# Turning the packed down weights late: all tiles in batch 12, their scaling on GpSimd in the last three batches

## The chip, the cores and the metric

The kernel runs on one core of one Trainium2 chip. The metric is the device time of one execution in microseconds (us); the kernel before took 838.14 us as the median of three runs (835.20, 838.14 and 841.78). One profiled execution gives all rows below.

## What is computed

A gated cross-attention layer and a gated feed-forward layer over 16 batches of `[128, 512]` float32:

```python
x = x + tanh(g_xattn) * attention(layernorm(x), ctx)      # 8 heads, projections mix the 128 rows
x = x + tanh(g_ffn) * ffn(layernorm(x))                   # 512 -> 2 x 1408 -> 512, then RMS norm

nib  = packed >> (4 * arange(8)) & 15                     # 8 weights of 4 bits in a word
vals = FP4_LUT[nib]                                       # 0, .5, 1, 1.5, 2, 3, 4, 6 and their negatives
w    = vals * repeat(scales, 128)                         # one fp16 scale per output and 128 inputs
h = silu(x @ w_gate.T) * (x @ w_up.T);  y = h @ w_down.T
```

Only the dequantization of `w_down` (512 x 1408, as 11 tiles of 128 x 512) is touched. Its result, a rounded head `dn_head` and the rest `dn_rest`, is first read in the feed-forward part, after all attention is done.

## The kernel before, in words

Two blocks run one after the other, with a barrier of all engines between them: `attend` (batches 0 to 15, up to about 490 us) and `feed_forward` (4 groups of 4 batches, 11 tiles each, to the end). Each engine has its instructions in a fixed order, written out by hand; semaphores tie them together.

In `attend`, a batch is 16 slots. In slot s of batch b, TensorE computes scores of batch b + 1 (L437), which VectorE reduces to row maxima (L699, `maxima`), and at the same time the transposed scores of batch b (L449), which ScalarE exponentiates (L556), and their product with the values (L467). So VectorE's maxima are always one batch ahead. The score results go through two buffers in turn, so TensorE can be two scores ahead of VectorE at most. VectorE also turns the maxima into rows (`turn_max`, L705, L707, L711) in slot 0 and slot 7, inverts the softmax sums of the batch before in slot 6 (`invert_sums`, L716), and in batch 15, in which it has no maxima, turns the gate and up weights in slots 1 to 6 (six operations of 1408 words, L720, L724, L728).

SyncE issues nearly all transfers, in one written order per batch (`sync_step`). Its late part matters here. In step b it stores the maxima of batch b (L260), loads them back (L266), gathers the sums of batch b - 1 (L274) and merges its quads (L280), then `store_x(b - 2)` (L298), which waits until the residual of batch b - 2 is added, then `store_inverse(b - 1)` (L285), `store_max(b + 1, 0)` (L260), its load (L266), `load_inverse(b - 1)` (L291), and `gather_sums(b, 0)` (L274). After step 15 come `gather_sums(15, 1)`, `merge_quads(15)`, `store_x(14)`, `store_inverse(15)`, `load_inverse(15)`, `store_x(15)`. What stands behind a waiting transfer in this order waits with it.

GpSimd runs `pool_step(b)`: `residual(b - 2)` (L662), the rotation and splitting of the projections of batch b + 3 while there are such (b below 13), `scale_heads(b - 1)` (L657), which waits for the inverse sums that SyncE loads (L291), and last `scale_down` for one tile. `residual(14)` stands after step 15; VectorE does batch 15's own.

The down weights travel so before: in batches 0 to 10 SyncE loads one tile of packed words (`load_down`, L348); in batches 1 to 11 it loads the tile's scales, spread over 128 partitions (`load_down_scale`, L303), into one of two buffers, and in slots 13 to 15 VectorE turns the bits of one tile, in three operations of 128 words (`turn_nibbles`): a shift of the upper half (L720), a mask and shift into `magnitude` (L724), a combination (L728). After that an fp8 view of the words gives the values. In steps 2 to 12 GpSimd does `scale_down` of one tile: product with the scales (L837), cast to the head (L839), the rest (L841).

Of the kernel before, what the change touches and what calls it, by code (L numbers as in the profile page):

```python
# [7 lines left out]
ALU = mybir.AluOpType  # L8
# [5 lines left out]
F16 = mybir.dt.float16  # L14
# [3 lines left out]
P = 128  # L18
B = 16
T = 512  # L20
# [5 lines left out]
IT = INNER // P  # L26
# [13 lines left out]
GU_COLS = 2 * INNER  # L40
GU_WORDS, DN_WORDS = KT * GU_COLS // 4, IT * T // 4
BIT_STEPS = 3
DN_AT, GU_AT = 2, 3
X_GAIN = 2.0 ** 11

SLOTS = 2 * QUADS * KT
# [51 lines left out]
def attend(nc, d, keep):  # L98
    with ExitStack() as ctx:
        sb = lambda name, shape, dt: ctx.enter_context(nc.sbuf_tensor(name, shape, dt))  # L100
        ps = lambda name, shape, dt: ctx.enter_context(nc.psum_tensor(name, shape, dt))
        sem = lambda name: ctx.enter_context(nc.semaphore(name))
        two = range(2)
# [36 lines left out]
        gu_bits, dn_bits = keep["gu_bits"], sb("dn_bits", [P, DN_WORDS], U32)  # L140
        magnitude = sb("magnitude", [P, DN_WORDS], U32)
        gu_sc16 = sb("gu_sc16", [P, KT, GU], F16)
        dn_sc16 = [sb(f"dn_sc16_{p}", [P, T], F16) for p in two]
        dn_full = sb("dn_full", [P, T], F32)

        st_ps = [ps(f"st_ps{r}", [P, T], F32) for r in range(ST_BANKS)]
# [9 lines left out]
        scales_in = sem("scales_in")  # L156
        gu_in = sem("gu_in")
        dn_in = sem("dn_in")
        dn_sc_in = [sem(f"dn_sc_in{p}") for p in two]
        x_in = [sem(f"x_in{n}") for n in range(X_TILES)]  # L160
        c_in = [sem(f"c_in{n}") for n in range(C_TILES)]
        consts = sem("consts")
# [3 lines left out]
        dn_turned = sem("dn_turned")  # L166
        gu_turned = sem("gu_turned")
        dn_product = sem("dn_product")
# [40 lines left out]
        turn = lambda n: n // 2 + 1  # L209
# [4 lines left out]
        with nc.Block() as block:  # L214
# [83 lines left out]
                sp.dma_start(keep["x_dram"][b], xt[b % X_TILES][:]).then_inc(x_stored[b % 2], 16)  # L298

            def load_down_scale(sp, t):  # L300
                if t >= 2:
                    sp.wait_ge(dn_product, t - 1)
                sp.dma_start(dn_sc16[t % 2][:], d["down_scales"][t].rearrange("(a h) -> a h", a=1).to_broadcast([P, T])).then_inc(dn_sc_in[t % 2], 16)  # L303

            def sync_step(sp, b):
                nxt, proj_n = b + 1 < B, b + AHEAD_PROJ
# [368 lines left out]
            def head_rot(dve, n):  # L675
                dve.wait_ge(rotated, n + 1)
                if n:
                    dve.wait_ge(stored[0], PARTS * n)
                nc.vector.tensor_copy(split_head[:, 0], swap[:]).then_inc(rot_head, 1)
# [7 lines left out]
            def take_v(dve, n):  # L687
                item = S_NO["v", n]
                dve.wait_ge(s_full, item + 1)
                if n >= 2:  # L690
                    dve.wait_ge(pv_done, (n - 1) * SPANS)
                out = v_ones[n % 2][:].rearrange("p k j q (a c) -> p (k j) (q a) c", a=2)[:, :, 0:4:3, :]
                nc.vector.tensor_copy(out, s_ps[item % S_BANKS][:, 0, :].rearrange("p (x q c) -> p x q c", q=QUADS, c=KC)).then_inc(s_read, 1)

            def maxima(dve, n, slot):
                item = S_NO["score", n, slot]
                j, qt = score_of(slot)
                dve.wait_ge(s_full, item + 1)
                nc.vector.tensor_reduce(neg_max[j // 2][:, :, j % 2, qt], s_ps[item % S_BANKS][:], AXIS_X, ALU.max,  # L699
                                        negate=True).then_inc(s_read, 1)  # L700

            def turn_max(dve, n, h):
                dve.wait_ge(s_read, S_NO["score", n, (h + 1) * SLOTS // QUADS - 1] + 1)
                maximum = neg_max[h][:].rearrange("p o j k -> p (o j k)")
                nc.vector.tensor_copy(max_rows[h][:, 0], maximum).then_inc(max_head[h], 1)  # L705
                dve.wait_ge(max_head[h], n + 1)
                nc.vector.tensor_tensor(max_rows[h][:, 1], maximum, max_rows[h][:, 0].bitcast(F32), ALU.subtract).then_inc(max_rest[h], 1)  # L707
                dve.wait_ge(max_rest[h], n + 1)
                if n:
                    dve.wait_ge(max_out[h], 16 * n)  # L710
                nc.vector.transpose(max_lines[h][:].bitcast(F32), max_rows[h][:].bitcast(F32).rearrange("p r i -> p (r i)")).then_inc(max_line[h], 1)  # L711

            def invert_sums(dve, b):
                for h in two:
                    dve.wait_ge(sums_in[h], 16 * (b + 1))
                nc.vector.reciprocal(sums[:], sums[:]).then_inc(inverses, 1)  # L716

            def turn_nibbles(dve, words, step, at, done, turned):
                if step == 0:
                    nc.vector.tensor_scalar(words[halves[0], at], words[halves[0], at], 4, None,  # L720
                                            ALU.logical_shift_left).then_inc(turned, 1)
                elif step == 1:
                    dve.wait_ge(turned, done + 1)
                    nc.vector.tensor_scalar(magnitude[:, 0:at.stop - at.start], words[:, at], 0x70707070, 1, ALU.bitwise_and,  # L724
                                            ALU.logical_shift_right).then_inc(turned, 1)
                else:
                    dve.wait_ge(turned, done + 2)
                    nc.vector.scalar_tensor_tensor(words[:, at], words[:, at], 0x80808080, magnitude[:, 0:at.stop - at.start],  # L728
                                                   ALU.bitwise_and, ALU.bitwise_or).then_inc(turned, 1)

            def vector_step(dve, b):
                proj_n = b + AHEAD_PROJ
                for slot in range(SLOTS):
                    if b + 1 < B:
                        maxima(dve, b + 1, slot)
                        if slot == V_AT:
                            take_v(dve, b + 1)
                    elif 1 <= slot <= 2 * BIT_STEPS:
                        if slot == 1:
                            dve.wait_ge(gu_in, 16 * 2 * KT)  # L740
                        piece, step = divmod(slot - 1, BIT_STEPS)
                        turn_nibbles(dve, gu_bits, step, slice(piece * DN_WORDS, (piece + 1) * DN_WORDS), BIT_STEPS * piece, gu_turned)
                    if slot == 0:
                        turn_max(dve, b, 1)
                    if slot == 3 and b + 4 < B:
                        statistics(dve, b + 4)
                    if slot == 6 and b:
                        invert_sums(dve, b - 1)
                    if slot == 7 and b + 1 < B:
                        turn_max(dve, b + 1, 0)  # L750
                    if slot == 7 and proj_n < B:
                        head_pass(dve, proj_n)
                    if slot == 11 and proj_n < B:
                        head_rot(dve, proj_n)
                    if slot >= SLOTS - BIT_STEPS and 1 <= b <= IT:
                        t = b - 1
                        dve.wait_ge(dn_in, 32 * b)
                        turn_nibbles(dve, dn_bits, slot - (SLOTS - BIT_STEPS), slice(t * T // 4, b * T // 4), BIT_STEPS * t, dn_turned)

            @block.vector  # L760
            def _(dve):
# [52 lines left out]
            def pool_step(pool, b):  # L814
                proj_n = b + AHEAD_PROJ
                if b >= 2:
                    residual(pool, nc.gpsimd, b - 2)
                if proj_n < B:
                    rotate_own(pool, nc.gpsimd, proj_n)
                    rotate_partner(pool, nc.gpsimd, proj_n)  # L820
                    rest_pass(pool, nc.gpsimd, proj_n)
                if b + 4 < B:
                    normalise(pool, nc.gpsimd, b + 4)
                if proj_n < B:
                    rest_rot(pool, nc.gpsimd, proj_n)
                if b:
                    scale_heads(pool, nc.gpsimd, b - 1)
                if DN_AT <= b < DN_AT + IT:
                    scale_down(pool, b - DN_AT)

            def scale_down(pool, t):
                pool.wait_ge(dn_turned, BIT_STEPS * (t + 1))
                if t:
                    pool.wait_ge(dn_rested, t)
                pool.wait_ge(dn_sc_in[t % 2], turn(t) * 16)
                vals = dn_bits[:].bitcast(FP8E3)[:, t * T:(t + 1) * T]
                nc.gpsimd.tensor_tensor(dn_full[:], vals, dn_sc16[t % 2][:], ALU.mult).then_inc(dn_product, 1)  # L837
                pool.wait_ge(dn_product, t + 1)
                nc.gpsimd.tensor_copy(keep["dn_head"][:, t, :], dn_full[:]).then_inc(dn_headed, 1)  # L839
                pool.wait_ge(dn_headed, t + 1)  # L840
                nc.gpsimd.tensor_tensor(keep["dn_rest"][:, t, :], dn_full[:], keep["dn_head"][:, t, :].bitcast(F32),  # L841
                                        ALU.subtract).then_inc(dn_rested, 1)
# [454 lines left out]
```

## Time and profile before

| | |
|---|---|
| median of 3 runs | 838.14 us (835.20 to 841.78) |
| profiled execution, its own time | 833.57 us |
| span of its instructions | 831.8 us |
| TensorE busy | 719.3 us (86%) |
| VectorE busy | 622.9 us (75%) |
| ScalarE busy | 531.9 us (64%) |
| GpSimd busy | 376.5 us (45%) |
| mean granted TensorE clock | 0.93 of full speed |

TensorE is busy nearly throughout, but "busy" includes matmuls that wait for the pace of others. Shares over the span mix two blocks with different limits, so the stretches below are cut at the starts of TensorE's first score (L437) of a batch: batch 3 starts at 131.81 us, batch 7 at 242.92, batch 8 at 267.98, batch 9 at 300.23, batch 12 at 382.52, batch 13 at 407.67, batch 14 at 431.57, batch 15 at about 454. The attention's last store is issued at 490.03 us, and the feed-forward block's first load at 490.77 us.

### The profile page before, as it was taken

How to read it: one execution, taken by the hardware profiler on the slowest of the kernel's cores; microseconds unless marked ns; L12 is line 12 of the kernel's file. 1: busy time of each engine (PE TensorE's matmuls, PEld its weight loads, DVE VectorE, ACT ScalarE, POOL GpSimd, SP SyncE). 2: the span in 40 equal slices, each digit the busy share in tenths (PEclk: the TensorE clock that was granted, in tenths of full speed). 3: DMA queues.
4: the chain of work that ended last, by engine and by line, in shares of the span. 5: the costliest groups of instructions: out<-in, count | busy, mean ns of one | idle time of the engine just before them, and what ended most of it. 6: DMA issues, size and time to landing. Idle time of an engine off the chain costs nothing. (4 is left out here: it accounts for less than half of the span.)

```text
span 831.8 us, 13555 instructions
## 1 busy us (share of the span) xinstructions
PE 719.3 (86%) x4660; PEld 338.8 (41%) x4660; DVE 622.9 (75%) x879; ACT 531.9 (64%) x965; POOL 376.5 (45%) x298
## 2 busy tenths in 40 slices
PE   3369999889999999999999805998998999889995
PEld 1124334333334334333344303554554555555553
DVE  5588999979889869898999316766677677776774
ACT  2217888768868658788788805565566457465744
POOL 2123344445444425454401102676558655955662
PEclk9559999999989859999999957999999999999999
DMA  6655677766776666666632140000000200000011
GB/s 212 196 154 164 148 191 199 203 158 179 197 215 184 160 172 172 165 184 183 177 95 63 38 159 36 1 0 2 1 0 26 77 0 1 27 25 1 1 39 63
DMA packets 55113, 88.74 MB, mean 107 GB/s; under 512 B 16901, under 2 KB 20357, under 8 KB 55045
## 3 DMA queue, kind: packets, MB, share of 16 engines
q1 hardware_dynamic: 54320, 87.68, 37.9%
q8 instruction: 37, 0.61, 0.3%
q10 hardware_dynamic: 724, 0.20, 0.1%
q14 instruction: 32, 0.25, 0.1%
HBM read 46.95 MB, written 34.34 MB: 98 GB/s over the span
## 5 line engine op out<-in xcount | busy, mean ns | idle before, releaser
L556 ACT ACTIVATE probs<-st_ps 128x512 f32<-128x512 f32 x512 | 277.2, 595 | 108.9 <-PE st_ps L449 97.9
L699 DVE TENSOR_REDUCE neg_max<-s_ps 128x2 f32<-128x1024 f32 x256 | 303.8, 1214 | 38.3 <-PE s_ps L437 37.7
L1075 POOL TENSOR_TENSOR pair<-parts 128x512 f32<-128x512 f32 x88 | 116.3, 1325 | 135.7 <-ACT parts L1095 135.7
L467 PE MATMUL pv_ps<-probs,v_ones 128*32 128x256 f32 x2048 | 168.9, 403 | 0.8 <-ACT pv_sb L562 0.8
L437 PE MATMUL s_ps<-k_stack,q_stack 48*128 48x512 f32 x512 | 137.3, 533 | 34.5 <-DVE neg_max L699 29.4
L1200 PE MATMUL gu_ps<-x_head,gu_bits 128*128 128x512 f16 x352 | 136.3, 387 | 19.3 <-ACT parts L1095 16.8
L1200 PE MATMUL gu_ps<-x_rest,gu_bits 128*128 128x512 f16 x352 | 135.4, 385 | 0.0
L1095 ACT ACTIVATE parts<-gu_ps,gu_sc 128x512 f32<-128x512 f32 x176 | 111.5, 680 | 10.6 <-PE gu_ps L1200 10.6
L449 PE MATMUL st_ps<-q_stack,k_stack 50*128 50x512 f32 x512 | 112.1, 424 | 0.0
L437 PEld LDWEIGHTS s_ps<-k_stack,q_stack 48*128 48x128 f32 x512 | 50.9, 196 | 148.8 <-DVE neg_max L699 72.5
L962 DVE SCALAR_TENSOR_TENSOR up<-gu_ps,gu_sc,up 128x512 f32<-128x512 f32 x132 | 98.6, 747 | 8.0 <-PE gu_ps L1200 4.2
L1102 ACT ACTIVATE silu<-gate 128x512 f32<-128x512 f32 x44 | 27.7, 630 | 109.7 <-POOL gate L1079 109.6
L959 DVE TENSOR_SCALAR up<-gu_ps,gu_sc 128x512 f32<-128x512 f32 x44 | 33.0, 751 | 68.4 <-PE gu_ps L1200 68.3
L467 PEld LDWEIGHTS pv_ps<-probs,v_ones 128*32 128x32 f32 x2048 | 41.1, 109 | 102.1 <-ACT probs L556 75.9
L1216 PE MATMUL y_ps<-dn_head,h_head 128*128 128x512 f32 x176 | 77.5, 440 | 4.4 <-DVE y_sb L1011 3.9
L1200 PEld LDWEIGHTS gu_ps<-x_head,gu_bits 128*128 128x128 fp8e3 x352 | 34.5, 98 | 86.3 <-ACT parts L1095 35.4
L1216 PE MATMUL y_ps<-dn_rest,h_head 128*128 128x512 f32 x176 | 69.4, 395 | 0.0
L1216 PE MATMUL y_ps<-dn_head,h_rest 128*128 128x512 f32 x176 | 69.3, 394 | 0.0
L449 PEld LDWEIGHTS st_ps<-q_stack,k_stack 50*128 50x128 f32 x512 | 63.9, 194 | 9.7 <-issue 4.4
L1079 POOL TENSOR_TENSOR gate<-pair 128x512 f32<-128x512 f32 x44 | 58.9, 1339 | 3.5
L657 POOL TENSOR_TENSOR heads_out<-pv_sb,scale_of 128x512 f32<-128x512 f32 x15 | 19.4, 1295 | 84.3 <-DMA scale_of<-inverse_scratch 84.3
L1200 PEld LDWEIGHTS gu_ps<-x_rest,gu_bits 128*128 128x128 fp8e3 x352 | 34.9, 99 | 30.7 <-issue 1.9
(109 smaller groups left out, 816.2 us busy)
## 6 DMA issues: line engine op xcount, KB each, us to landing
q_stack<-image SPq DMA_DIRECT2D x64, 192.0 KB, 3.5
k_stack<-image SPq DMA_DIRECT2D x64, 192.0 KB, 4.5
image<-split_head SPq DMA_DIRECT2D x32, 256.0 KB
image<-split_head SPq DMA_DIRECT2D x64, 128.0 KB
image<-split_rest SPq DMA_DIRECT2D x32, 256.0 KB
ct<-ctx_dram SPq DMA_DIRECT2D x16, 256.0 KB, 6.3
swap<-proj SPq DMA_DIRECT2D x64, 64.0 KB, 2.7
scale_of<-inverse_scratch SPq DMA_DIRECT2D x16, 256.0 KB
```

The source lines that it names most:

```text
L437: last = nc.tensor.matmul(out[:, odd, :], q_stack[p][rows, j, qt * P:(qt + 1) * P], k_stack[p][rows, j, :], start=True, stop=True)
L449: nc.tensor.matmul(out[:], k_stack[p][rows, j, kt * P:(kt + 1) * P], q_stack[p][rows, j, :], start=True, stop=True).then_inc(st_full, 1)
L467: last = nc.tensor.matmul(pv_ps[2 * KC * j:2 * KC * (j + 1), cols], v_ones[b % 2][:, kt, j, quad, :], probs[at % PROBS][:, j, cols], start ...
L556: nc.scalar.activation(probs[at % PROBS][:, tile % 4, :], st_ps[item % ST_BANKS][:], ACT.Exp).then_inc(st_read, 1)
L699: nc.vector.tensor_reduce(neg_max[j // 2][:, :, j % 2, qt], s_ps[item % S_BANKS][:], AXIS_X, ALU.max, negate=True).then_inc(s_read, 1)
L959: nc.vector.tensor_scalar(out, bank, scale, None, ALU.mult).then_inc(up_read, 1)
L962: nc.vector.scalar_tensor_tensor(out, bank, scale, out, ALU.mult, ALU.add).then_inc(up_read, 1)
L1075: nc.gpsimd.tensor_tensor(pair[:, n], parts[T_ % 2][:, 2 * n], parts[T_ % 2][:, 2 * n + 1], ALU.add).then_inc(pairs_ok, 1)
L1079: nc.gpsimd.tensor_tensor(gate[T_ % 2][:], pair[:, 0], pair[:, 1], ALU.add).then_inc(gate_ok, 1)
L1095: nc.scalar.activation(parts[T_ % 2][:, k], gu_ps[(2 * k) % BANKS][:], ACT.Copy, scale=gu_sc[:, k, T_ % IT:T_ % IT + 1]).then_inc(gate_rea ...
L1200: last = nc.tensor.matmul(gu_ps[n % BANKS][:], gu_vals[:, k, col:col + P], moving[g % 2][:, k], start=first, stop=not first)
L1216: last = nc.tensor.matmul(y_ps[:, j, :], h[T_ % H_RING][:, cols], keep[w][:, t, :], start=(t == 0 and n == 0), stop=(t == IT - 1 and n == 2))
```

## The change

The words of all 11 tiles stay packed until slots 13 to 15 of batch 12, where three operations turn them all (1408 words each). GpSimd scales and splits four tiles in step 13, four in step 14 and three in step 15, each time after `scale_heads`. The scales of all tiles get a buffer of their own, so loading them waits for nothing; the loads keep their places in SyncE's order.

```diff
-DN_AT, GU_AT = 2, 3
+DN_AT, DN_TILES, GU_AT = 13, 4, 3
...
-        dn_sc16 = [sb(f"dn_sc16_{p}", [P, T], F16) for p in two]
+        dn_sc16 = sb("dn_sc16", [P, IT, T], F16)
...
             def load_down_scale(sp, t):
-                if t >= 2:
-                    sp.wait_ge(dn_product, t - 1)
-                sp.dma_start(dn_sc16[t % 2][:], d["down_scales"][t].rearrange("(a h) -> a h", a=1).to_broadcast([P, T])).then_inc(dn_sc_in[t % 2], 16)
+                sp.dma_start(dn_sc16[:, t, :], d["down_scales"][t].rearrange("(a h) -> a h", a=1).to_broadcast([P, T])).then_inc(dn_sc_in, 16)
...
-                    if slot >= SLOTS - BIT_STEPS and 1 <= b <= IT:
-                        t = b - 1
-                        dve.wait_ge(dn_in, 32 * b)
-                        turn_nibbles(dve, dn_bits, slot - (SLOTS - BIT_STEPS), slice(t * T // 4, b * T // 4), BIT_STEPS * t, dn_turned)
+                    if slot >= SLOTS - BIT_STEPS and b == DN_AT - 1:
+                        dve.wait_ge(dn_in, 32 * IT)
+                        turn_nibbles(dve, dn_bits, slot - (SLOTS - BIT_STEPS), slice(0, DN_WORDS), 0, dn_turned)
...
-                if DN_AT <= b < DN_AT + IT:
-                    scale_down(pool, b - DN_AT)
+                if b >= DN_AT:
+                    for t in range(DN_TILES * (b - DN_AT), min(IT, DN_TILES * (b - DN_AT + 1))):
+                        scale_down(pool, t)
...
             def scale_down(pool, t):
-                pool.wait_ge(dn_turned, BIT_STEPS * (t + 1))
+                pool.wait_ge(dn_turned, BIT_STEPS)
                 if t:
                     pool.wait_ge(dn_rested, t)
-                pool.wait_ge(dn_sc_in[t % 2], turn(t) * 16)
+                pool.wait_ge(dn_sc_in, 16 * (t + 1))
                 vals = dn_bits[:].bitcast(FP8E3)[:, t * T:(t + 1) * T]
-                nc.gpsimd.tensor_tensor(dn_full[:], vals, dn_sc16[t % 2][:], ALU.mult).then_inc(dn_product, 1)
+                nc.gpsimd.tensor_tensor(dn_full[:], vals, dn_sc16[:, t, :], ALU.mult).then_inc(dn_product, 1)
```

## Rows read from the trace of the kernel before

**Rows 1.** Windows by batch: stretch, its us, busy by engine, clock, DMA share, GB/s

```profile
131.81:382.52 250.71, 235.92 (x1894) 94.07 (x1890) 216.20 (x289) 187.53 (x352) 114.31 (x100) 0.93 0.68 183
242.92:267.98 25.06, 24.37 (x214) 9.90 (x211) 22.91 (x33) 20.80 (x40) 12.09 (x11) 1.00 0.65 186
267.98:300.23 32.25, 30.50 (x215) 11.51 (x211) 25.69 (x33) 21.27 (x41) 14.97 (x13) 0.78 0.73 193
382.52:407.67 25.15, 24.33 (x214) 9.72 (x211) 22.62 (x28) 20.51 (x38) 11.85 (x10) 1.00 0.61 169
407.67:431.57 23.90, 22.25 (x206) 9.50 (x203) 22.16 (x25) 19.12 (x36) 6.39 (x6) 1.00 0.49 124
```

**Rows 2.** Groups of instructions of VectorE: the turning of one tile, eleven times

```profile
L728 DVE SCALAR_TENSOR_TENSOR dn_bits<-dn_bits,magnitude 128x128 uint32<-128x128 uint32 x11 | 4.5, 407 | 0.0
L724 DVE TENSOR_SCALAR magnitude<-dn_bits 128x128 uint32<-128x128 uint32 x11 | 3.4, 308 | 0.0
L720 DVE TENSOR_SCALAR dn_bits<-dn_bits 64x128 uint32<-64x128 uint32 x11 | 2.3, 208 | 0.0
```

**Rows 3.** Timeline, VectorE and GpSimd, slot 0 of batch 13: start, us, what

```profile
408.79 1.28 POOL L657 TENSOR_TENSOR heads_out<-pv_sb,scale_of 128x512 f32<-128x512 f32 x1 [4.57 <-DMA scale_of<-inverse_scratch]
409.36 0.74 DVE L705 CAST max_rows<-neg_max 128x16 fp32r<-128x16 f32 x1
410.03 1.10 POOL L837 TENSOR_TENSOR dn_full<-dn_bits,dn_sc 128x512 f32<-128x512 fp8e3 x1
410.13 1.03 DVE L707 TENSOR_TENSOR max_rows<-neg_max,max_rows 128x16 fp32r<-128x16 f32 x1
411.19 0.61 POOL L839 CAST dn_head<-dn_full 128x512 fp32r<-128x512 f32 x1
411.19 0.21 DVE L711 STREAM_TRANSPOSE max_lines<-max_rows 128x32 f32<-128x32 f32 x1
411.88 1.28 POOL L841 TENSOR_TENSOR dn_rest<-dn_full,dn_head 128x512 fp32r<-128x512 f32 x1
```

**Rows 4.** Timeline, VectorE, slot 0 of batch 14

```profile
433.67 0.21 DVE L711 STREAM_TRANSPOSE max_lines<-max_rows 128x32 f32<-128x32 f32 x1
```

**Rows 5.** Waits: who waited for what, us in total, times, longest

```profile
DVE sums L716 <- DMA sums<-pv_sb: 18.2, 6, 14.1
```

**Rows 6.** Timeline, VectorE and GpSimd, batch 15: turning 1408 words of `gu_bits`

```profile
455.41 0.84 DVE L720 TENSOR_SCALAR gu_bits<-gu_bits 64x1408 uint32<-64x1408 uint32 x1
457.22 1.62 DVE L728 SCALAR_TENSOR_TENSOR gu_bits<-gu_bits,magnitude 128x1408 uint32<-128x1408 uint32 x1
459.67 0.89 DVE L724 TENSOR_SCALAR magnitude<-gu_bits 128x1408 uint32<-128x1408 uint32 x1
460.30 1.40 POOL L662 TENSOR_TENSOR xt<-xt,attn 128x512 f32<-128x512 f32 x1 [9.00 <-ACT attn L571]
460.60 2.59 DVE L728 SCALAR_TENSOR_TENSOR gu_bits<-gu_bits,magnitude 128x1408 uint32<-128x1408 uint32 x1
```

**Rows 7.** Timeline, GpSimd and SyncE's queue, from step 13's end to the attention's end

```profile
430.70 1.28 POOL L657 TENSOR_TENSOR heads_out<-pv_sb,scale_of 128x512 f32<-128x512 f32 x1 [14.16 <-DMA scale_of<-inverse_scratch]
443.86 0.50 SPq L260 DMA_DIRECT2D max_scratch<-max_lines  x1
446.43 0.64 SPq L291 DMA_DIRECT2D scale_of<-inverse_scratch  x1
450.02 1.28 POOL L657 TENSOR_TENSOR heads_out<-pv_sb,scale_of 128x512 f32<-128x512 f32 x1 [10.63 <-DMA scale_of<-inverse_scratch]
469.55 1.28 POOL L657 TENSOR_TENSOR heads_out<-pv_sb,scale_of 128x512 f32<-128x512 f32 x1 [7.85 <-DMA scale_of<-inverse_scratch]
478.91 0.52 SPq L298 DMA_DIRECT2D x_scratch<-x_last  x1
479.48 1.24 SPq L285 DMA_DIRECT2D inverse_scratch<-sums  x2
481.93 0.64 SPq L291 DMA_DIRECT2D scale_of<-inverse_scratch  x1
```

More of the change, by code:

```diff
@@ L158, in attend @@
         dn_in = sem("dn_in")
-        dn_sc_in = [sem(f"dn_sc_in{p}") for p in two]
+        dn_sc_in = sem("dn_sc_in")
         x_in = [sem(f"x_in{n}") for n in range(X_TILES)]
```

## The prediction

> **What bounds the kernel now.** I read the 40 slices of the profile first (they show where attention ends and the feed-forward block starts), then the windows cut at each batch, then the timeline of VectorE, GpSimd and SyncE's queue around the lines that move. The change touches nothing after 490.77 us, where the feed-forward block starts; all of its effect is on when attention ends.
>
> In the windows an undisturbed batch takes 25.06 us, and batch 12, in which VectorE turns no down weights at all, takes 25.15 us [rows 1]. So in an undisturbed batch the turning is worth nothing: TensorE and ScalarE set a slot's pace, and VectorE's three small operations fit in front of the next score. But nine batches (3 to 11) take 250.71 us together, 25.2 us more than 9 x 25.06; batch 8 alone takes 32.25 us at a granted clock of 0.78, a mixture of both levels, 1.2 and 2.4 GHz [rows 1]. In these VectorE waits in slot 6 for the sums that SyncE gathers [rows 5], scores pile up, and the clock falls behind such a gap.
>
> At the other end, after batch 13, GpSimd has almost nothing to do, but what it does stands on a chain: residual, `store_x`, `store_inverse`, `load_inverse`, `scale_heads`, one turn per batch, because SyncE issues in a fixed order. In the last turn the inverse of batch 15 is issued right behind `store_x(14)` (478.91, then 479.48), and everything to the end of attention hangs on it [rows 7].
>
> **The change, part by part.**
>
> *Removed from VectorE in batches 1 to 11:* 33 operations, 2.3 + 3.4 + 4.5 = 10.2 us busy [rows 2]. Taken at nothing directly, covered by the score's own pace as said.
>
> *Removed from GpSimd in steps 2 to 12:* eleven tiles. GpSimd had time for them, but they got in VectorE's way. In slot 0 of batch 13 a cast that should be short took 0.74 us, ending with GpSimd's L657, and the subtraction L707 took 1.03 us, ending as L837 ends; the transpose L711 started 3.52 us after the batch, against 2.10 us (433.67 - 431.57) in batch 14, where GpSimd was idle [rows 1, 3, 4]. So up to 1.42 us came off the store of the maxima in each such batch, and behind this store stands the gathering of the sums. The bounds: a gain of nothing, if the landing of the transfers decides (SyncE issues as many as before), and of all 25.2 us, if every disturbed batch becomes an undisturbed one. I take 4.1 us, the five waits for sums during the loop (18.2 - 14.1, the last being the wait at the end) [rows 5], because a store that is at most 1.4 us earlier reaches that far and no further: **-4.1**.
>
> *Loads of scales:* as many, at the same places in SyncE's order; the wait that goes was for a product two batches old. Nothing.
>
> *Added to VectorE in slots 13 to 15 of batch 12:* three operations of the size of the gate and up turns: 0.84 (L720), 0.89 (L724) and 1.62 us (L728), 3.35 us; up to 1 us more if GpSimd is in the way, as in the L728 that took 2.59 us [rows 6]. A maximum behind each of them waits, and with two score buffers TensorE is held soon after. Batch 13 no longer has the 1.42 us of interference, of which the part by `scale_heads` (about 0.6 us) stays [rows 3]. Nothing later in the loop gives the delay back, since TensorE's slot is then no shorter: 3.35 - 0.85 = **+2.5** (bounds +1.5 and +4.5: part of it hidden by the buffers, or both blockings in full).
>
> *Added to GpSimd in steps 13 to 15:* tiles. One costs by the spacing of starts 1.16 + 0.69, then 1.28 and the gap to the next, which I estimate from the two earlier gaps at 0.07: 3.20 us [rows 3]. Now the chain on the old clock times [rows 3, 6, 7]:
> - `scale_heads(12)` at 430.70, first tile 1.24 us later, four tiles to 444.7, then `residual(12)` to 446.0. SyncE's `store_x(12)` waits for it, and behind it `store_inverse(13)` (0.57 + 1.24), `store_max(15, 0)` and from there 2.57 us to `load_inverse(13)`: 450.4. It was 446.43.
> - `scale_heads(13)` 3.59 us later, at 454.0 (was 450.02). Four tiles: 1.24 + 12.8, to 468.1 if undisturbed.
> - These run just when VectorE turns the gate and up weights. GpSimd's L662 began at 460.30 while VectorE's L724 ran until 460.56, and took 1.40 us where its kind takes 1.28; the L728 behind it stood until GpSimd had finished (2.59 us against 1.62) [rows 3, 6]. So they take turns, and each VectorE operation that runs holds GpSimd for its length less about 0.13. Six of them, 2 x 3.35 = 6.7, less 0.8: 5.9 us more, to 474.0. `residual(13)` to 475.3.
> - `store_x(13)` 475.3, to `load_inverse(14)` 3.02 us (478.91 to 481.93), 478.3; `scale_heads(14)` 3.59 later, 481.9; three tiles, 1.24 + 9.6, to 492.8; `residual(14)` to 494.1, `store_x(14)` at 494.1. It was at 478.91: **+15.2**.
>
> VectorE and TensorE have room behind this chain: the merges of batch 15 were issued before `store_x(14)` at 478.91, so even 5 us later they don't decide. What is late next is only `store_inverse(15)` itself.
>
> The Trainium skill (SBUF — State Buffer, Who interferes with whom) has the loser of the port pair that GpSimd and VectorE share block fully, for the whole instruction of the other. By the rule six whole operations, 6.7 us, would be added instead of 5.9, and the sum would be 0.8 us higher; the trace agrees in kind and is a little milder.
>
> The Trainium skill (Perfetto Trace Analysis, the notes under the GPSIMD instruction) warns that a GpSimd span in a profile is unreliable and that start-to-start spacing is to be used. By the spans (1.10 + 0.61 + 1.28) a tile would be 2.99 us, and eleven tiles 2.3 us less than by the spacing that I take.
>
> **Sum.** -4.1 + 2.5 + 15.2 = +13.6 us. On the profiled execution's own 833.57 us this is 847.2. That execution was faster than all three runs shown, whose median is 838.14; on that it is 851.7. I predict against the median: **851 us**.
>
> **Rivals.**
> - *The turns don't hold GpSimd.* If VectorE's six operations fit beside the tiles, or fall before them, the last term is 15.2 - 5.9 = 9.3 and the sum +7.7: 846 us. Against it is the 1.40 us row; for it, that it is one row with an overlap of 0.26 us [rows 6]. Chance 0.2.
> - *The loop gives back more than the tail takes.* The mechanism: in slot 0 of batches 3 to 12 the maxima leave up to 1.42 us sooner, the sums are there in slot 6, and neither the wait nor the fall of the clock behind it comes. If all 25.2 us go: +17.7 - 25.2 = -7.5, 831 us. It decides where more than 17.7 of the 25.2 us come back. For it: the undisturbed batches show that the clock is whole (1.00) wherever VectorE doesn't stall [rows 1]. Against: SyncE has no transfer less to issue. Chance 0.12.
> - *A fall of the clock more.* VectorE's 3.35 us in batch 12 hold TensorE longer than any wait in rows 5 but the last; if the clock falls as in batch 8, whose excess over 25.06 was 7.2 us, and half to all of this comes on top: +17 to +21, 857 us. Chance 0.1.
> - *The change moves nothing of weight*, because the tail is covered by something later than the sums' inverse: I see nothing there; 838 us. Chance 0.03.
>
> My forecast has 0.55.
>
> **How the numbers follow.** The forecast's own range is 847 to 856 (recovery of 0 to 8 us, the turn between +1.5 and +4.5). The range to the first and third rival is 840 to 858; left out are the second and fourth rival and something above. A measurement of this kernel tells about 1% (8.4 us) from no change. Slower by more than that, above 846.5: nearly all of the forecast, half of the first rival, the third: 0.72. Faster, below 829.8: only the second rival at its very end, 0.04. Within: 0.24.
>
> **What would show it.** In the profile after: L716 no longer waits in the loop, and the batches 3 to 12 are shorter by some us in all; three long VectorE operations in batch 12 and TensorE waiting for L699 there; GpSimd without a gap from its L657 in steps 13, 14 and 15 through the tiles; its operations in batch 15 lengthened beside L720, L724 and L728; `store_x(13)` and `store_x(14)` waiting for GpSimd's L662, the latter about 15 us later than the end of the merges would allow; the feed-forward stretch as long as before. I am wrong if `store_x(14)` doesn't wait, or if batches 3 to 12 shrink by 10 us and more.

## The result

The changed kernel is slower: 859.10 us median (854.76 to 862.93, four runs) against 839.96 us (835.20 to 842.29, four runs), a ratio of 1.0234 with a 95% interval of 1.0158 to 1.0309. That is 19 us where 13 were forecast, 1.1 us above the end of the range. The kernel before has one execution more here than when the prediction was made, and its median is 1.8 us higher for it. Here and below, medians take in every execution, while ratios leave out the slow ones, those more than 1.5% above the fastest of their kernel. The changed kernel's profiled execution took 854.76 us, its span is 852.6 us against 831.8.

### The profile page after: what moved, and what is told of

It is laid out like the page before. It is cut to its first block and busy times, and to the rows that moved or that the text cites. A ratio compares the mean times of both kernels' runs of the same rounds, so it can differ in the third digit from the quotient of the medians.

```text
span 852.6 us, 13505 instructions
## 1 busy us (share of the span) xinstructions
PE 728.8 (85%) x4660; PEld 342.5 (40%) x4660; DVE 620.9 (73%) x849; ACT 531.3 (62%) x965; POOL 381.1 (45%) x298
## 5 line engine op out<-in xcount | busy, mean ns | idle before, releaser
L1093 ACT ACTIVATE parts<-gu_ps,gu_sc 128x512 f32<-128x512 f32 x176 | 111.5, 678 | 11.6 <-PE gu_ps L1198 11.5
L435 PEld LDWEIGHTS s_ps<-k_stack,q_stack 48*128 48x128 f32 x512 | 51.2, 197 | 152.0 <-issue 73.0
L655 POOL TENSOR_TENSOR heads_out<-pv_sb,scale_of 128x512 f32<-128x512 f32 x15 | 19.6, 1308 | 81.3 <-DMA scale_of<-inverse_scratch 81.3
```

What stands on the lines that cost most here:

```text
L435: last = nc.tensor.matmul(out[:, odd, :], q_stack[p][rows, j, qt * P:(qt + 1) * P], k_stack[p][rows, j, :], start=True, stop=True)
L1093: nc.scalar.activation(parts[T_ % 2][:, k], gu_ps[(2 * k) % BANKS][:], ACT.Copy, scale=gu_sc[:, k, T_ % IT:T_ % IT + 1]).then_inc(gate_rea ...
```

## The profile after

The same stretches as in [rows 1], from the changed kernel's windows (stretch, us, busy by engine, clock, DMA share, GB/s): batches 3 to 11, and batch 13.

```profile
132.52:385.19 252.67, 237.85 (x1894) 95.13 (x1890) 208.93 (x262) 187.23 (x352) 86.81 (x72) 0.91 0.71 182
410.38:437.10 26.72, 23.95 (x203) 9.73 (x203) 23.43 (x27) 18.99 (x35) 3.00 (x2) 0.94 0.45 111
```

GpSimd did 86.8 us of work in batches 3 to 11 instead of 114.3, and VectorE 208.9 instead of 216.2, but they took 252.67 us instead of 250.71 [rows 1]. Batch 13 took 26.72 us instead of 23.90.

The chain at the end, which answers to [rows 7] (timeline, GpSimd and SyncE's queue; L655 is `scale_heads`, L660 the residual, L298 `store_x`):

```profile
437.13 1.28 POOL L655 TENSOR_TENSOR heads_out<-pv_sb,scale_of 128x512 f32<-128x512 f32 x1 [15.25 <-DMA scale_of<-inverse_scratch]
451.39 1.29 POOL L660 TENSOR_TENSOR xt<-xt,attn 128x512 f32<-128x512 f32 x1
460.55 1.28 POOL L655 TENSOR_TENSOR heads_out<-pv_sb,scale_of 128x512 f32<-128x512 f32 x1 [7.87 <-DMA scale_of<-inverse_scratch]
479.28 1.28 POOL L660 TENSOR_TENSOR xt<-xt,attn 128x512 f32<-128x512 f32 x1
487.23 1.26 POOL L655 TENSOR_TENSOR heads_out<-pv_sb,scale_of 128x512 f32<-128x512 f32 x1 [6.67 <-DMA scale_of<-inverse_scratch]
498.01 1.26 POOL L660 TENSOR_TENSOR x_last<-x_last,attn 128x512 f32<-128x512 f32 x1
...
499.30 0.34 SPq L298 DMA_DIRECT2D x_scratch<-x_last  x1
```

No residual here has an idle time in brackets: GpSimd came to each straight from a tile. From `scale_heads(12)` to `store_x(14)` it is 499.30 - 437.13 = 62.17 us; before it was 478.91 - 430.70 = 48.21 [rows 7].

The two engines beside each other in batch 15 (VectorE's turning of the gate and up weights, and GpSimd's tiles, in two answers of the timeline):

```profile
463.08 1.21 DVE L718 TENSOR_SCALAR gu_bits<-gu_bits 64x1408 uint32<-64x1408 uint32 x1
464.33 1.86 DVE L722 TENSOR_SCALAR magnitude<-gu_bits 128x1408 uint32<-128x1408 uint32 x1
466.22 2.41 DVE L726 SCALAR_TENSOR_TENSOR gu_bits<-gu_bits,magnitude 128x1408 uint32<-128x1408 uint32 x1
468.56 1.29 DVE L718 TENSOR_SCALAR gu_bits<-gu_bits 64x1408 uint32<-64x1408 uint32 x1
...
463.63 1.80 POOL L839 TENSOR_TENSOR dn_rest<-dn_full,dn_head 128x512 fp32r<-128x512 f32 x1
465.57 1.58 POOL L835 TENSOR_TENSOR dn_full<-dn_bits,dn_sc 128x512 f32<-128x512 fp8e3 x1
467.21 1.89 POOL L837 CAST dn_head<-dn_full 128x512 fp32r<-128x512 f32 x1
469.18 1.82 POOL L839 TENSOR_TENSOR dn_rest<-dn_full,dn_head 128x512 fp32r<-128x512 f32 x1
```

A cast of 0.61 us takes 1.89, a product of 1.10 takes 1.58, a rest of 1.28 takes 1.80 (the shorter ones in [rows 3]), and the VectorE operations are longer than the undisturbed ones in [rows 6] too: the six together run from 463.08 to 474.20, 11.1 us for what takes 6.7 alone.

The whole difference of 20.8 us of span, cut at the same events in both traces (one execution of each kernel, so that the loop's row, above all, holds their spread too):

| stretch | before, us | after, us | difference | forecast |
|---|---|---|---|---|
| to batch 3 | 131.81 | 132.52 | +0.7 | 0 |
| batches 3 to 11 | 250.71 | 252.67 | +2.0 | -4.1 |
| batch 12 to `scale_heads(12)` | 48.18 | 51.94 | +3.8 | +2.5 |
| `scale_heads(12)` to `store_x(14)` | 48.21 | 62.17 | +14.0 | +15.2 |
| to the feed-forward's first load | 11.86 | 11.68 | -0.2 | 0 |
| feed-forward | 341.03 | 341.62 | +0.6 | 0 |

## The experiments

Two theories stood after the result. **A**: the loss is the long turn in batch 12 and the tail, and the loop (batches 3 to 11) gains nothing because something in SyncE's or the DMA engines' work sets its pace. **D**: taking GpSimd's tiles out of the loop is worth the 4.1 us forecast, and something else loses more. Ratios are to the kernel before, on the same chip.

**Turning early, scaling late**

```diff
-                    if slot >= SLOTS - BIT_STEPS and b == DN_AT - 1:
-                        dve.wait_ge(dn_in, 32 * IT)
-                        turn_nibbles(dve, dn_bits, ..., slice(0, DN_WORDS), 0, dn_turned)
+                    if slot >= SLOTS - BIT_STEPS and 1 <= b <= IT:
+                        t = b - 1
+                        dve.wait_ge(dn_in, 32 * b)
+                        turn_nibbles(dve, dn_bits, ..., slice(t * T // 4, b * T // 4), BIT_STEPS * t, dn_turned)
```

> The changed kernel, but VectorE turns one tile in each of batches 1 to 11 as before (slots 13 to 15), and only GpSimd's scaling is late. Theory A (the loss has two places: the three long VectorE operations in batch 12 cost 3.7 us up to scale_heads(12), and GpSimd's tiles ahead of the residuals cost 14 us behind it): about 4 us less than the changed kernel, so 15 to 16 us over the kernel before, 855 us; batch 13 back at about 24 us. Rival B (the long operations only fill a gap in VectorE, the loss is all in the tail): no different from the changed kernel, 859 us. Rival C (turning per batch costs time in the loop, which the change had saved): slower than the changed kernel, 861 us or more.

Measured: 860.0 us, ratio 1.0207 (1.0116 to 1.0298): the time alone doesn't tell it from the changed kernel. Its windows do:

```profile
135.55:400.24 264.69, 249.32 (x1894) 97.16 (x1890) 211.33 (x289) 187.31 (x352) 86.72 (x72) 0.86 0.66 173
425.73:448.43 22.70, 22.18 (x206) 9.60 (x203) 20.74 (x25) 18.91 (x36) 3.29 (x3) 1.00 0.50 130
```

Batch 13 took 22.70 us, 4.0 less than with the late turn, but this execution's loop took 12 us more, at a clock of 0.86. The loop varies by more than the term that I wanted to see. Whether turning per batch makes it longer (rival C) this run leaves open; it stands against it that of f1 and f2 below, which both have the same loads moved, the one that turns per batch (f2) has the shorter loop, 244.1 us against 254.2.

**The same tiles, in GpSimd's gaps**

```diff
+                for t in {14: (2, 3), 15: (7, 8)}.get(b, ()):
+                    scale_down(pool, t)
                 if b:
                     scale_heads(pool, nc.gpsimd, b - 1)
-                if b >= DN_AT:
-                    for t in range(DN_TILES * (b - DN_AT), min(IT, DN_TILES * (b - DN_AT + 1))):
-                        scale_down(pool, t)
+                for t in {13: (0, 1), 14: (4, 5, 6), 15: (9, 10)}.get(b, ()):
+                    scale_down(pool, t)
```

> The changed kernel with the same eleven late tiles on GpSimd in another order: two after scale_heads(12), then residual(12), two, scale_heads(13), three, residual(13), two, scale_heads(14), two, residual(14). No residual then waits for more than one or two tiles. Theory A: the chain residual, store_x, store_inverse, load_inverse, scale_heads is nearly free again; of the 14 us behind scale_heads(12) at most 3 stay (two tiles before scale_heads(13) and (14), each stretched by VectorE's turning of the gate and up weights), so about 12 us less than the changed kernel, 5 to 7 us over the kernel before, 846 us. Rival B (GpSimd's total work late is what costs, wherever it stands): 857 us, as the changed kernel.

Measured: 848.18 us, ratio 1.0080 (1.0037 to 1.0123). 1.5% of the 2.3% came back without a tile less: most of what costs is where the tiles stand in the order, not GpSimd's work. From `scale_heads(12)` to `store_x(14)` it was 52.64 us:

```profile
435.32 1.28 POOL L655 TENSOR_TENSOR heads_out<-pv_sb,scale_of 128x512 f32<-128x512 f32 x1 [14.76 <-DMA scale_of<-inverse_scratch]
...
487.96 0.34 SPq L298 DMA_DIRECT2D x_scratch<-x_last  x1
```

**No work on the down weights.** The kernel leaves out the turning and the scaling and fills the weights with a constant, so its result is not the layer's; the loads stay.

```diff
-                        turn_nibbles(dve, dn_bits, ..., slice(0, DN_WORDS), 0, dn_turned)
...
-                        scale_down(pool, t)
+                if b < 2:
+                    nc.gpsimd.memset(keep[("dn_head", "dn_rest")[b]][:].bitcast(F32), 0.25).then_inc(dn_product, 1)
```

> The changed kernel without the turning and the scaling of the down weights: dn_head and dn_rest are filled with a constant by two memsets of GpSimd in steps 0 and 1, the loads of words and scales stay. It bounds what all this work costs. Theory A (in the kernel before, the work was free, because SyncE's issuing sets the pace of batches 3 to 11): the time of the kernel before within 2 us, 838 to 842 us. Rival D (the step of the prediction: interference of GpSimd with VectorE in slot 0 cost 4.1 us): 4 us less than the kernel before, 836 us. With the changed kernel as measure, 18 to 20 us less by A, 23 by D.

Measured: ratio 0.9993 (0.9938 to 1.0049); the median of all ten executions is 848.92 us against 841.87. In the kernel before, turning and scaling cost nothing that this run can tell from zero. The interval reaches 5.2 us down, so it does not by itself exclude D's 4.1.

**Gate and up loads out of the loop** (on the kernel before)

```diff
-                if GU_AT <= b < GU_AT + 2 * KT:
-                    load_gate_up(sp, b - GU_AT)
+                if b in (12, 13):
+                    for n in range(4 * (b - 12), 4 * (b - 11)):
+                        load_gate_up(sp, n)
```

> The kernel before with one thing changed: the eight loads of packed gate and up weights leave steps 3 to 10 of SyncE's order and stand in steps 12 and 13, four each, where SyncE has fewer transfers to issue. Theory A (in batches 3 to 10 SyncE's issue of about 42 transfers, some 25.7 us, and their landing are what makes every second batch late): each batch gains about 0.6 us of issue and the queue ahead of the maxima is shorter, so the long batches mostly vanish; 5 to 20 us less than the kernel before, 828 us. Rival E (the long batches come from VectorE's and GpSimd's work, not from SyncE): no change, 838 to 841 us.

Measured: 830.55 us, ratio 0.9879 (0.9787 to 0.9971). Moving eight transfers that nobody waits for until batch 15 gains what moving eleven tiles of real work did not:

```profile
135.59:377.75 242.16, 227.64 (x1890) 90.71 (x1890) 218.65 (x288) 186.65 (x350) 113.56 (x99) 0.96 0.69 182
```

The loop took 242.16 us instead of 250.71, with one long fall of the clock left (batch 6, 32.6 us), and VectorE's waits for the sums in it come to 0.5 us instead of 4.1:

```profile
DVE sums L717 <- DMA sums<-pv_sb: 14.6, 2, 14.1
```

**The changed kernel in the calmer loop, and both mends there.** The first is the changed kernel with the edit of the last experiment; the second has besides the early turn of the first and the gaps of the second experiment.

> The changed kernel with the gate and up loads in steps 12 and 13, as in e4_gate_up_loads_late, to whose 830.6 us it is to be compared: the loop varies less there. Theory A (the loss is the long turn in batch 12, 3.7 to 4.8 us, and the tail behind scale_heads(12), 14 us): 18 us over e4, 849 us; from scale_heads(12) to store_x(14) 62 us against 46.6 in e4. Rival F (part of the loss measured for the change is more falls of the clock in the loop, which the calmer loop doesn't have): 13 us over e4 or less, 843 us.

Measured: ratio 1.0124 (1.0071 to 1.0177), 850.57 us. From `scale_heads(12)` (444.82) to `store_x(14)` (507.02) it was 62.20 us, as A said. Its profiled execution was the longest of its ten, 861.69 us.

> As f1_after_calm, with both mends: VectorE turns one tile per batch in batches 1 to 11, and GpSimd's tiles stand in its gaps, as in e2_tiles_in_gaps. Theory A (two places, additive): of the 18 us the turn's 4 and 10 of the tail's 14 come back, 835 us, 4 to 5 over e4. Rival C (turning one tile per batch costs the loop what the late turn saves): 839 us.

Measured: ratio 0.9946 (0.9905 to 0.9988), 836.62 us. The two mends together are worth 1.8%, and 14 us by the medians of the two, where A said 14. From `scale_heads(12)` (429.80) to `store_x(14)` (479.20) it was 49.40 us. Batch 13 of the two (f1, then f2):

```profile
415.94:443.49 27.55, 25.12 (x203) 10.04 (x204) 23.53 (x27) 19.07 (x36) 2.59 (x2) 0.88 0.60 147
...
404.30:427.55 23.25, 22.27 (x208) 9.52 (x204) 20.84 (x25) 18.90 (x36) 2.56 (x2) 1.00 0.69 168
```

Again about 4 us for the late turn, and with it the clock below 1. Batch 7 of f1 took 31.26 us at a clock of 0.82 although VectorE did not wait in its slot 6: a late sum is not the only thing that stands before a fall. Rival F is not confirmed: against e4's ratio of 0.9879, f1 is 2.5% slower, no less than the change cost at first.

**The gate and up turn after the tiles** (on the changed kernel)

```diff
+                dve.wait_ge(gu_in, 16 * 2 * KT)
+                dve.wait_ge(dn_rested, 8)
+                for n in range(2 * BIT_STEPS):          # after batch 15's slots, not in slots 1 to 6
+                    piece, step = divmod(n, BIT_STEPS)
+                    turn_nibbles(dve, gu_bits, step, slice(piece * DN_WORDS, (piece + 1) * DN_WORDS), ...)
```

> The changed kernel, but VectorE turns the gate and up weights after batch 15's slots, once GpSimd has finished eight tiles, instead of beside tiles 4 to 7. Theory A (the two engines take turns, so six VectorE operations lengthen GpSimd's tiles): the four tiles 4 to 7 take 13 us instead of 17.5, and the time from scale_heads(12) to store_x(14) is 57.5 us instead of 62.2. Rival (they don't block each other, the tiles are long for another reason): 17 us and 62 us as before.

Measured in a single execution, 852.75 us (timeline, GpSimd):

```profile
463.82 1.28 POOL L655 TENSOR_TENSOR heads_out<-pv_sb,scale_of 128x512 f32<-128x512 f32 x1 [7.88 <-DMA scale_of<-inverse_scratch]
477.97 1.28 POOL L660 TENSOR_TENSOR xt<-xt,attn 128x512 f32<-128x512 f32 x1
```

`scale_heads(13)`, its four tiles and the start of the residual took 14.15 us, against 18.73 us in the changed kernel (479.28 - 460.55); from `scale_heads(12)` (440.39) to `store_x(14)` (497.89) it was 57.50 us, against 62.17. So 4.6 us of the tail were VectorE and GpSimd in each other's way. The time of the whole tells nothing here.

**Fewer transfers, same bytes in all** (on e4)

```diff
-                if b < IT:
-                    load_down(sp, b)
-                if 1 <= b <= IT:
-                    load_down_scale(sp, b - 1)
+                if b == 0:
+                    load_down(sp)                       # all words, two transfers
+                if b in (1, 4, 8):
+                    load_down_scales(sp, {1: 0, 4: 4, 8: 8}[b])
```

> The kernel before with the gate and up loads in steps 12 and 13 and the down weights' transfers merged: all packed words in two transfers in step 0 (22 before), the scales in three, in steps 1, 4 and 8 (11 before); turning and scaling as in the kernel before. Theory A (SyncE's issuing and the queue it fills pace batches 2 to 11): SyncE then has slack in every batch, nearly all take 25.1 us, and it is 5 to 12 us under e4's 830.6: 821 us. Rival G (what is left in e4 above 25.1 us a batch is GpSimd's tiles in slot 0, up to 0.7 us each, not SyncE): 2 us under e4 at most, 829 us.

Measured: ratio 0.9904 (0.9830 to 0.9978), no better than e4's 0.9879; the median of all ten executions is 839.69 us against 841.96. I was wrong here: 28 transfers fewer for SyncE to issue gained nothing that shows. That speaks against the number of issues in theory A. It is no support for the bytes either, because batches 3 to 11 lost all words of the down weights and, except for steps 4 and 8, the scales too.

**Scales out of the loop too** (on f2)

```diff
-                if 1 <= b <= IT:
-                    load_down_scale(sp, b - 1)
+                if b in (12, 13):
+                    for t in range(6 * (b - 12), min(IT, 6 * (b - 11))):
+                        load_down_scale(sp, t)
```

> As f2_calm_both_mended (0.9946 of the kernel before, 836.6 us), but the eleven loads of the down scales, 128 KB each, stand in steps 12 and 13 too. Theory A2 (what decides batches 3 to 11 is how many bytes the DMA engines, 90 to 100% busy in the 10 us around each batch's start, still have ahead of the stored maxima): eight loads of 176 KB moved gave 10 us, so eleven of 128 KB give about as much again, at least 5 us: 829 us. Rival H (only the number of transfers that SyncE issues counts; one fewer per batch): as merging them in f4_down_loads_merged, 2 us or less: 835 us.

Measured: ratio 0.9915 (0.9846 to 0.9985) against f2's 0.9946 (0.9905 to 0.9988). The intervals overlap: inconclusive between A2 and H. By the medians of all executions (839.04 us against 839.71, and f2's 836.62 against 841.96) g1 is not even the better one. Its batch 11 took 30.46 us at a clock of 0.81 with no wait in slot 6. Its batch 13 took 33.21 us:

```profile
399.58:432.79 33.21, 30.61 (x206) 11.98 (x202) 21.76 (x25) 19.41 (x37) 6.93 (x7) 0.71 0.75 176
```

Ten of the moved loads now stand in SyncE's order just ahead of that batch's maxima. VectorE had turned these 2.5 us after the batch's start, but the store was issued at 5.2 us and the load back at 11.5, and in slot 6 VectorE waited 3.95 us for the sums. Part of what the loop got rid of is paid here.

**The maxima's way out of SyncE's queue** (on e4, then on the changed kernel)

```diff
-                store_max(sp, b, 1)
                 if nxt:
                     load_half(sp, b + 1, 1)
-                load_max(sp, b, 1)
...
+                    if slot == 1:
+                        store_max(act, b, 1)
+                    if slot == 4:
+                        load_max(act, b, 1)
```

> The kernel of e4_gate_up_loads_late (0.988 of the kernel before), but the store of the second half of the maxima and its load back are issued by ScalarE's queue (in slots 1 and 4) and not by SyncE's, so SyncE's swap and gathering of the sums don't wait for that store to land. Theory A2 (VectorE's wait in slot 6, and the falls of the clock behind it, come from that wait of SyncE's queue): no L717 wait in the loop, nearly all batches near 25.2 us, 5 to 10 us under e4: 823 us. Rival I (the sums land late anyway, because the same engines are full): no different from e4, 830 us; or slower, if ScalarE's issuing takes more than its 0.15 us of slack in a slot.

Measured: 825.89 us, ratio 0.9874 (0.9784 to 0.9964); by ratio no better than e4, whose own interval is as wide. The trace shows the mechanism, in the window of batches 3 to 11 and in the waits (L719 is the inversion of the sums, and its one wait is that at the attention's end):

```profile
137.31:372.05 234.74, 224.67 (x1891) 91.57 (x1890) 215.16 (x289) 184.25 (x352) 113.76 (x99) 1.00 0.70 189
...
DVE sums L719 <- DMA sums<-pv_sb: 14.1, 1, 14.1
```

The wait of slot 6 is gone from every batch of the loop, no batch shows a fall of the clock (1.00 over all nine), and the loop is 16 us shorter than in [rows 1], 7.4 of them against e4's, whose waits were down to 0.5 us already. ScalarE now waits for the maxima itself; what that costs in all isn't measured:

```profile
193.38 1.08 ACT L555 ACTIVATE probs<-st_ps 128x512 f32<-128x512 f32 x2 [0.84 <-DVE max_lines L714]
```

> The changed kernel (859 us, 1.023 of the kernel before) with that same move of the maxima to ScalarE's queue and nothing else. Theory A2: the loop (batches 3 to 11, 252.7 us in the changed kernel's profile) loses 10 us or more, the long turn and the tail stay (batch 13 near 26.7 us, 62 us from scale_heads(12) to store_x(14)): 847 us. Rival I: 859 us.

Measured: 855.56 us, ratio 1.0192 (1.0008 to 1.0375), which the time alone doesn't tell from the changed kernel's 1.0234. This pair differs in the maxima's queue and in nothing else, and VectorE's waits for the sums in the loop fell from 6.4 us to 11.2 - 10.9 = 0.3. The loop took 245.64 us, 7 us less than in the changed kernel and not 10. Batch 5 still took 31.38 us at a clock of 0.80, with no wait in slot 6; batch 13, with the long turn, fell to a clock of 0.73 in this execution and gave 5 us back:

```profile
DVE sums L716 <- DMA sums<-pv_sb: 11.2, 2, 10.9
...
186.56:217.94 31.38, 29.74 (x214) 11.56 (x211) 24.21 (x30) 21.20 (x41) 10.92 (x9) 0.80 0.75 207
133.15:378.79 245.64, 232.65 (x1895) 93.07 (x1891) 212.35 (x262) 186.03 (x352) 86.89 (x72) 0.94 0.70 186
403.98:436.07 32.09, 29.73 (x202) 10.83 (x202) 23.98 (x27) 19.00 (x36) 4.98 (x5) 0.73 0.33 92
```

**All mends together.** g1 with the maxima on ScalarE's queue.

> The kernel of g1_scales_late_too (GpSimd's tiles late, in its gaps; VectorE turns one tile per batch; gate and up words and down scales loaded in steps 12 and 13) with the maxima's second half stored and loaded by ScalarE's queue, as in g2_maxima_on_scalar_queue. It asks whether taking GpSimd's tiles out of the loop is worth something once the sums don't come late. Theory J (the prediction's step, right once the landing is out of the way: the turned maxima leave about 0.6 us sooner in slot 0, and ScalarE waits less for them): the loop, batches 3 to 11, is 3 to 5 us shorter than g2's 234.7, against 3 us more behind scale_heads(12) for the tiles in the gaps: equal to g2, 826 us, 0.984 of the kernel before. Rival K (the tiles in the loop cost nothing at all): loop of 234 us, 829 us.

Measured: 826.94 us against 846.70 us of the kernel before on this chip, ratio 0.9811 (0.9745 to 0.9877), the best ratio of all, and so a version that beats both kernels. Its loop:

```profile
136.88:365.40 228.52, 220.49 (x1894) 89.61 (x1890) 209.02 (x289) 185.21 (x352) 86.70 (x72) 1.00 0.67 188
```

228.52 us is 25.39 a batch, close to the undisturbed 25.06, and 6.2 us less than g2's. The transpose of the maxima starts 2.86 us after a batch's start on the mean of the nine, against 3.47 in g2: the 0.6 us of J, and a batch is 0.7 us shorter. So this is what moving the tiles could give. But g2 keeps the loads of scales in the loop and h1 doesn't, so how much of the 6.2 us is GpSimd's absence and how much the bytes isn't separated. And h1 pays in batch 13 as g1 did, with the moved loads ahead of the sums and 3.0 us of waiting in slot 6:

```profile
390.95:419.77 28.82, 26.62 (x207) 10.87 (x204) 21.25 (x25) 18.96 (x36) 4.97 (x5) 0.82 0.76 194
```

## Why the prediction was wrong

**The step that failed is the first term, -4.1 us** for GpSimd's tiles leaving the loop, because "a store that is at most 1.4 us earlier reaches that far". The store did leave earlier, on the mean of batches 3 to 11 by 0.8 us (2.63 after a batch's start instead of 3.42), but the load back, which waits until it has landed, only by 0.2 (6.60 instead of 6.80). Batch 3, in the kernel before and then in the changed one (timelines, SyncE's queue; L266 is the load back), shows it most clearly:

```profile
135.67 0.58 SPq L260 DMA_DIRECT2D max_scratch<-max_lines  x1
139.18 0.52 SPq L266 DMA_DIRECT2D q_stack<-max_scratch  x2
...
134.85 0.59 SPq L260 DMA_DIRECT2D max_scratch<-max_lines  x1
139.99 0.52 SPq L266 DMA_DIRECT2D q_stack<-max_scratch  x2
```

Counted from the batch's start (131.81 and 132.52), the store went out at 3.86 and then at 2.33 us, and the load back followed at 7.37 and at 7.47. The 16 KB stand behind what SyncE issued just ahead of them (image tiles, inputs, words, scales). The ten microseconds around that batch's start, in windows of before and of after:

```profile
129.30:139.30 10.00, 9.80 (x84) 3.78 (x82) 9.93 (x14) 9.03 (x17) 4.26 (x4) 1.00 0.84 246
...
129.50:139.50 10.00, 10.00 (x88) 3.71 (x86) 9.18 (x11) 9.18 (x17) 1.28 (x1) 1.00 0.95 256
```

The DMA engines are 84% and 95% busy there, and the earlier store waited longer. Behind the load back stand SyncE's swaps and the gathering of the sums, and VectorE waits for these in slot 6. The waits in the changed kernel's loop (all but the last and longest, at the attention's end) are 19.6 - 13.2 = 6.4 us, against 4.1 before [rows 5], where the prediction expected none:

```profile
DVE sums L714 <- DMA sums<-pv_sb: 19.6, 5, 13.2
```

The prediction named this bound itself ("a gain of nothing, if the landing of the transfers decides") and then took 4.1. Four more profiles without GpSimd's tiles in the loop, with SyncE's order as it was, had loops of 249.1 (e2), 252.5 (f3), 257.9 (e3) and 264.7 us (e1), none clearly below 250.7, and waits for the sums in them of 4.2, 6.6, 6.6 and 7.7 us. g3 and g2, which take the maxima's store and load back out of SyncE's order and change nothing else, show that SyncE's wait for the landing was what made the sums late: 6.4 us of waiting became 0.3, and 0.5 became none. How much of the whole time hangs on it they don't show, since neither ratio differs clearly from that of the kernel it was made from.

Two things stay open. Why the landing is late in some batches: e4 moved 176 KB a batch and gained, and g1 and h1 lost time in batch 13, where they had put bytes, but f4 and g1 as wholes gained nothing that shows, and the share of the DMA engines alone doesn't tell. In the changed kernel's batch 5 the engines were 96% busy, and the load back was issued 3.1 us behind the store, nearly as soon as SyncE's four loads between them let it:

```profile
187.20:197.20 10.00, 10.00 (x86) 3.86 (x82) 9.06 (x13) 9.05 (x17) 1.42 (x2) 1.00 0.96 253
```

And why the clock falls: in the kernel before, each fall has such a wait in its batch or in the one ahead, as the prediction read it, but batch 7 of f1, batch 5 of g3 and batch 11 of g1 fell to 0.82, 0.80 and 0.81 without one.

**The long turn** was forecast at +2.5 and measured at +3.8 in this pair. The three operations took 3.37 us, as forecast:

```profile
408.22 0.88 DVE L718 TENSOR_SCALAR dn_bits<-dn_bits 64x1408 uint32<-64x1408 uint32 x1
410.16 0.88 DVE L722 TENSOR_SCALAR magnitude<-dn_bits 128x1408 uint32<-128x1408 uint32 x1
412.09 1.61 DVE L726 SCALAR_TENSOR_TENSOR dn_bits<-dn_bits,magnitude 128x1408 uint32<-128x1408 uint32 x1
```

What was missed is small: batch 13 runs at a clock of 0.94 after them, 0.88 in f1, 0.73 in g3. In the five profiles with the long turn it took 26.7 to 27.6 us and once 32.1; without it 22.7 to 24.8, except in g1 and h1 (33.2 and 28.8), where the moved loads stand ahead of it. It was the third rival's mechanism, at a fraction of its price in most profiles.

**The tail** was right by its own steps. Forecast from `scale_heads(12)`, and measured: `scale_heads(13)` 23.3 and 23.4 us, `scale_heads(14)` 51.2 and 50.1, `store_x(14)` 63.4 and 62.2. The 1.2 us too much are the turns with VectorE: 5.9 forecast, 4.6 by f3. The Trainium skill's rule (SBUF — State Buffer, Who interferes with whom: the loser blocks fully) would have given 6.7. The direction agrees with the rows, and the measured cost to GpSimd is less than the sum of VectorE's lengths; VectorE lost about as much, 11.1 us for 6.7 of work. Why the two together lose less than the whole of both isn't shown. The first rival, no turns at all, is refuted by f3.

**The second rival**, that the loop gives back more than the tail takes, did not come; h1 shows that its size was real (22.2 us less than [rows 1]'s loop) but that GpSimd's tiles were not the lock on it.

**The range** ended at 858, too low for its own terms. The forecast's bounds, nothing for the loop and +4.5 for the turn, already make 838.1 + 19.7 = 857.8 where "847 to 856" was written, and the third rival's +21 makes 859. With the first term at nothing, 0 + 3.8 + 15.2 is 19.0, or 857 us on the median of before as it then was, just inside. That the result lies outside is owed to the 1.8 us by which that median rose; that the forecast was 6 us short is owed to the first term and, by 1.3 us, to the turn, with the tail 1.2 us the other way.

## What to carry to other kernels

Where a queue waits for a transfer to land, an earlier issue need not be an earlier landing: here 0.8 us at the store left 0.2 at the load back. Follow the chain to the step that is waited for before giving a gain to the engine that feeds it, and look whether the waiting can move to another queue. Bytes that nobody waits for yet can be moved away, but see what they stand ahead of in their new place. Work put "where an engine is idle" is free only between the chain's own steps on that engine: the same eleven tiles cost 14 us in front of three residuals and about 4 spread around them. Where a loop falls now and then to the lower clock, judge small terms by the windows of single batches, because the whole time hides them.

## What was not expected

The granted clock goes along with much of the spread from one execution of a kernel to the next: on one chip the kernel before took 835.57 us at a mean of 0.929 and 847.89 at 0.908, and this change's executions took 854.76 us at 0.906 and 862.93 at 0.901. In the profiles of e4, g2 and h1, in which transfers were moved and no arithmetic left out, it was 0.937, 0.941 and 0.938. One cast on GpSimd, 0.61 us alone, took 1.89 us when VectorE's operations of 1408 words stood beside it.
